# Spreading two small operands over the heads by one set of wide products instead of two sets of narrow ones

## The reference, cut to what matters

```
def _L0_xattn_ref(x, context, W_out, b_out, heads):
    q = x.reshape(b, i, heads, d).transpose(0, 2, 1, 3)
    k = context.reshape(b, j, heads, d).transpose(0, 2, 1, 3)
    v = k
    sim = jnp.einsum('bhid,bhjd->bhij', q, k) * scale
    attn = jax.nn.softmax(sim, axis=-1)
    out = jnp.einsum('bhij,bhjd->bhid', attn, v)
    ...
    return out @ W_out.T + b_out
x = x + _L0_xattn_ref(_layernorm(x, axis=-1), ctx_1024, ...)
x = x + _L0_attn_ref(_layernorm(x, axis=-1), ...)
x = x + _L0_ffn_ref(_layernorm(x, axis=-1), ...)
```

## Time and profile before

| | |
|---|---|
| median of 3 runs | 860.65 us (860.27 to 861.3) |
| the profiled execution | 856.09 us |
| its span, first to last instruction | 854.2 us |
| granted TensorE clock, mean | 0.985 |
| TensorE busy | 764.7 us (90%) |
| VectorE busy | 607.9 us (71%) |
| ScalarE busy | 422.8 us (49%) |
| GpSimd busy | 313.4 us (37%) |

### The profile page before, as it was taken

One profiled execution on the slowest core, in us unless ns is written; L12 is line 12 of the kernel. 1 busy time (PEld: TensorE's weight loads), 2 busy tenths in 40 slices (PEclk: granted clock), 3 DMA queues, 4 the chain that ended last, 5 costly groups with the idle time before them and its releaser, 6 DMA issues.

```text
span 854.2 us, 26663 instructions
## 1 busy us (share of the span) xinstructions
PE 764.7 (90%) x10666; PEld 573.3 (67%) x10666; DVE 607.9 (71%) x1211; ACT 422.8 (49%) x1062; POOL 313.4 (37%) x638
## 2 busy tenths in 40 slices
PE   4798879989898898989989898898988889999998
PEld 2445767768686776867768686786876655666664
DVE  3378687777878778787777877778645566878883
ACT  2344455564646555464564645555332255555552
POOL 2012523324233333333324233333320434786642
PEclk9899999999999999999999999999999899999999
DMA  9945665656547555474555537454061399454430
GB/s 283 316 109 119 140 145 116 141 133 152 137 107 180 125 153 139 109 176 117 137 140 143 140 110 175 125 156 107 3 222 45 129 377 394 159 186 140 143 115 4
DMA packets 113850, 129.17 MB, mean 151 GB/s; under 512 B 13950, under 2 KB 80766, under 8 KB 113728
## 3 DMA queue, kind: packets, MB, share of 16 engines
q1 hardware_dynamic: 105984, 109.35, 48.2%
q0 software_dynamic: 5520, 16.26, 5.6%
q10 hardware_dynamic: 2224, 1.86, 0.8%
HBM read 114.85 MB, written 14.42 MB: 151 GB/s over the span
## 4 chain that ended last, share of the span: by engine, by line
PE 59%; DVE 16%; POOL 7%; issue 7%; ACT 4%; DMA 4%; SPq 3%; DVEq 0%; POOLq 0%
PE bank L499 10%; PE bank L501 8%; PE bank L500 8%; PE bank L1559 8%; PE bank L493 4%; PE scores L550 3%; PE scores L540 3%; PE bank L564 2%; DVE negmax L1030 2%; PE scores L1537 2%; PE scores L1539 2%; PE scores L1538 2%; DMA keys<-in_ctx 2%; POOL soft L1314 2%; PE bank L604 2%
## 5 line engine op out<-in xcount | busy, mean ns | idle before, releaser
L825 ACT ACTIVATE prob<-scores,negmax 128x257 f32<-128x257 f32 x256 | 118.0, 476 | 41.5 <-DVE negmax L1030 40.8
L499 PE MATMUL bank<-qkv_hi,operand_hi 128*128 128x396 f32 x256 | 99.2, 387 | 4.3 <-DVE operand_lo L1034 4.2
L1030 DVE TENSOR_REDUCE negmax<-scores 128x2 f32<-128x514 f32 x128 | 82.1, 683 | 21.8 <-PE scores L540 21.8
L1020 DVE STREAM_TRANSPOSE k_t<-keys 128x512 f32<-128x512 f32 x128 | 88.2, 690 | 12.6 <-DMA keys<-in_ctx 12.5
L500 PE MATMUL bank<-qkv_lo,operand_hi 128*128 128x396 f32 x256 | 88.0, 344 | 0.0
L501 PE MATMUL bank<-qkv_hi,operand_lo 128*128 128x396 f32 x256 | 87.6, 342 | 0.0
L1559 PE MATMUL bank<-w_all,hidden 128*128 x184 | 82.8, 592 | 0.6 <-ACT hidden L1612 0.6
L550 PE MATMUL scores<-consts,prob 128*128 128x128 f32 x512 | 76.7, 273 | 1.6 <-ACT prob L825 1.6
L564 PEld LDWEIGHTS bank<-prob_t,context 128*32 128x32 f32 x4096 | 46.5, 112 | 42.5 <-issue 34.6
L1655 DVE TENSOR_TENSOR w_lo<-w_all,w_hi 128x512 fp32r<-128x512 f32 x89 | 69.2, 836 | 0.2
L550 PEld LDWEIGHTS scores<-consts,prob 128*128 128x128 f32 x512 | 62.5, 143 | 9.6 <-ACT prob L825 2.5
(11 more groups left out here) (249 smaller groups left out, 1718.5 us busy)
## 6 DMA issues: line engine op xcount, KB each, us to landing
keys<-in_ctx SPq DMA_DIRECT2D x256, 128.0 KB, 4.5
context<-in_ctx SPq DMA_DIRECT2D x64, 512.0 KB, 4.6
w_all<-in_L_ffn_W SPq DMA_DIRECT2D x16, 1024.0 KB, 12.8
b<-in_L_ffn_b SPq DMA_DIRECT2D x23, 256.0 KB, 3.6
norm_scratch<-norm SPq DMA_DIRECT2D x16, 256.0 KB, 2.0
x_tile<-in_x SPq DMA_DIRECT2D x8, 256.0 KB, 5.4
x_pair<-in_x SPq DMA_DIRECT2D x8, 256.0 KB, 4.6
x_scratch<-x_tile SPq DMA_DIRECT2D x8, 256.0 KB, 2.5
```

The lines of the kernel that those rows point to most:

```text
L499: pe.matmul(to, op_hi[op][:, c, :], w_hi[name][:, c, columns], start=(c == 0), stop=False)
L825: act.activation(prob[pair][:, gg, :], scores[:, g, 0:J], ACT.Exp, bias=negmax[b % 2][:, g:g + 1], accum_out=sums[t % 2][:, g, bl:bl + 1]) ...
L1020: dve.transpose(dst, src).then_inc(keys_turned, 1)
L1030: dve.tensor_reduce(negmax[b % 2][:, 2 * pair:2 * pair + 2], scores[:, 2 * pair:2 * pair + 2, 0:J], AX.X, ALU.max, negate=True).then_inc(m ...
```

## The change

The two operands of the spread are placed side by side in one tile, `op_both`, so that for each g the 128 columns of `op_plast` stand directly ahead of the 128 of `op_inv`. TensorE makes four products of 256 columns instead of eight of 128: g = 0 and 1 go into bank 0, g = 2 and 3 into bank 2, which is now the physical neighbour of bank 0, so that VectorE reads each half over both banks with one access pattern. One signal, `spread_done`, stands for both; `inv_spread` is gone, and with it VectorE's wait before L1069. The stage `SPREAD_INV` is gone, and `SPREAD` stands at offset 4 instead of 3. Bank 1 is no longer used by the spread. Bank 0 counts as empty once `att_used` is raised (by L1069) instead of `spread_used` (by L1061). GpSimd's `op_inv` waits once for the first bias unit, whose weights share the tile.

```
-    op_plast = late[:, 5, :].rearrange("p (g b i) -> p g b i", g=G, b=BT)
...
-    op_inv = staged_c[:, 0, :].rearrange("p (g b i) -> p g b i", g=G, b=BT)
+    op_both = staged_c[:, 0:2, :].rearrange("p k (g w b i) -> p (k g) w b i", w=2, b=BT, i=S)
+    op_plast, op_inv = op_both[:, :, 0, :, :], op_both[:, :, 1, :, :]
...
+    banks = [stage_banks[:, i, :] for i in (0, 2, 1)]
+    spread_plast, spread_inv = (stage_banks[:, 0:2, :].rearrange("p k (g w n) -> p (k g) w n", w=2, n=P)[:, :, w, :] for w in range(2))
...
-    bank_of = {"queries": 0, "spread": 0, ..., "inv": 1, ...}
+    bank_of = {"queries": 0, "spread": 0, ..., "inv": 2, ...}
...
-    emptied = {..., "spread": spread_used, "inv": att_used, ...}
+    emptied = {..., "spread": att_used, "inv": att_used, ...}
...
             t = tile_at(step, SPREAD)
             if t >= 0:
-                bank = bank_for("spread", t)
                 until.wait_ge(tables_made, 3)
                 until.wait_ge(plast_placed, t + 1)
-                for g in range(G):
-                    done = pe.matmul(bank[:, g * P:(g + 1) * P], samehead[:, g, :, :]...,
-                                     op_plast[:, g, :, :]..., start=True, stop=True)
-                done.then_inc(spread_done, 1)
-            t = tile_at(step, SPREAD_INV)
-            if t >= 0:
-                bank = bank_for("inv", t)
                 until.wait_ge(inv_placed, t + 1)
                 for g in range(G):
-                    done = pe.matmul(bank[:, g * P:(g + 1) * P], samehead[:, g, :, :]...,
-                                     op_inv[:, g, :, :]..., start=True, stop=True)
-                done.then_inc(inv_spread, 1)
+                    if g % 2 == 0:
+                        bank = bank_for(("spread", "inv")[g // 2], t)
+                    done = pe.matmul(bank[:, (g % 2) * 2 * P:(g % 2 + 1) * 2 * P], samehead[:, g, :, :]...,
+                                     op_both[:, g, :, :, :]..., start=True, stop=True)
+                done.then_inc(spread_done, 1)
...
-                dve.tensor_tensor(grid4(att_w), grid4(banks[bank_of["spread"]]), last, ALU.mult).then_inc(spread_used, 1)
+                dve.tensor_tensor(grid4(att_w), spread_plast.rearrange("p g (b i) -> p g b i", b=BT), last, ALU.mult).then_inc(spread_used, 1)
...
-                until.wait_ge(inv_spread, t + 1)
                 until.wait_ge(att_added, t + 1)
-                dve.tensor_tensor(att_w[:, :], att_w[:, :], banks[bank_of["inv"]][:, :], ALU.mult).then_inc(att_used, 1)
+                dve.tensor_tensor(split3(att_w), split3(att_w), spread_inv, ALU.mult).then_inc(att_used, 1)
...
                 until.wait_ge(inverted, t + 1)
-                until.wait_ge(inv_spread, t)
+                until.wait_ge(spread_done, t)
+                until.wait_ge(unit_done, UNITS.index(("bias", 0)) + 1)
```

More of the change, by code:

```diff
@@ L38 @@
 TILE = BT * STEPS
-(INVERT, PLACE_LAST, PLACE_INV, X_BIAS, SPREAD, SPREAD_INV, ATT, ATT_INV, ATT_HI, ATT_LO, XOUT, X1, SCALE1, TURN1, QKV, OUT_BIAS, TURN_Q, TURN_K,
+(INVERT, PLACE_LAST, PLACE_INV, X_BIAS, SPREAD, ATT, ATT_INV, ATT_HI, ATT_LO, XOUT, X1, SCALE1, TURN1, QKV, OUT_BIAS, TURN_Q, TURN_K,
  SELF, SOFT, SOFT_EXP, SOFT_SUM, SOFT_SCALE, SOFT_TURN, SOFT_PLACE, AV, OUT, X2, SCALE3, TURN3, GATE, CHOOSE, RANK,
  QUERIES) = (
-    -5, 0, -5, -6, 3, 3, 3, 4, 4, 2, 10, 17, 19, 21, 24, 26, 41, 41, 45, 46, 46, 50, 48, 56, 55, 63, 83, 89, 86, 95, 105, 105, 118, -54)
+    -5, 0, -5, -6, 4, 3, 4, 4, 2, 10, 17, 19, 21, 24, 26, 41, 41, 45, 46, 46, 50, 48, 56, 55, 63, 83, 89, 86, 95, 105, 105, 118, -54)
 MEASURE_X, SCALE_X = 2 * STEPS + 4, 2 * STEPS + 5
@@ L279, in program @@
     scores = ctx.enter_context(nc.psum_tensor("scores", [P, G, 512], F32))
-    psum = [ctx.enter_context(nc.psum_tensor(f"bank{i}", [P, 512], F32)) for i in range(4)]
-    att_bank, banks = psum[0], psum[1:4]
+    att_bank = ctx.enter_context(nc.psum_tensor("att_bank", [P, 512], F32))
+    stage_banks = ctx.enter_context(nc.psum_tensor("stage_banks", [P, 3, 512], F32))
+    banks = [stage_banks[:, i, :] for i in (0, 2, 1)]
+    spread_plast, spread_inv = (stage_banks[:, 0:2, :].rearrange("p k (g w n) -> p (k g) w n", w=2, n=P)[:, :, w, :] for w in range(2))
     def by_head(t_):
@@ L330, in program @@
     measured_x, rstd_x, normed_x = signal("measured_x"), signal("rstd_x"), signal("normed_x")
-    inverted, plast_placed, inv_placed, spread_done, inv_spread, spread_used, att_added, att_used = (
-        signal(n) for n in ("inverted", "plast_placed", "inv_placed", "spread_done", "inv_spread", "spread_used", "att_added", "att_used"))
+    inverted, plast_placed, inv_placed, spread_done, spread_used, att_added, att_used = (
+        signal(n) for n in ("inverted", "plast_placed", "inv_placed", "spread_done", "spread_used", "att_added", "att_used"))
     att_hi, att_lo = signal("att_hi"), signal("att_lo")
@@ L366, in emptied_unit @@
         return {"down": down_moved, "k": k_summed, "bias": bias_moved}[kind], c + 1
-    bank_of = {"queries": 0, "spread": 0, "xout": 0, "norm": 1, "qkv0": 1, "qkv2": 1, "out": 2, "inv": 1, "gate": 0, "av": 0, "qkv1": 2, "q": 1, "k": 0, "norm3": 1, "rank": 0, "qkv3": 0, "self": 1}
-    step_of = {"queries": QUERIES, "spread": SPREAD, "inv": SPREAD_INV, "xout": XOUT, "norm": TURN1, "qkv0": QKV, "qkv1": QKV + 4, "qkv2": QKV + 8, "qkv3": QKV + 12,
+    bank_of = {"queries": 0, "spread": 0, "xout": 0, "norm": 1, "qkv0": 1, "qkv2": 1, "out": 2, "inv": 2, "gate": 0, "av": 0, "qkv1": 2, "q": 1, "k": 0, "norm3": 1, "rank": 0, "qkv3": 0, "self": 1}
+    step_of = {"queries": QUERIES, "spread": SPREAD, "inv": SPREAD, "xout": XOUT, "norm": TURN1, "qkv0": QKV, "qkv1": QKV + 4, "qkv2": QKV + 8, "qkv3": QKV + 12,
                "q": TURN_Q, "k": TURN_K, "self": SELF, "av": AV, "out": OUT, "norm3": TURN3, "gate": GATE, "rank": RANK}
@@ L376, in stage_step @@
         return step_of[stage] + TILE * (t + 1) + (later_of.get(stage, (0, 0))[t - T + 2] if t >= T - 2 else 0)
-    emptied = {"queries": queries_placed, "spread": spread_used, "inv": att_used, "xout": x1_made, "norm": norm_lo, "q": q2_moved, "self": soft_shifted, "av": self_lo,
+    emptied = {"queries": queries_placed, "spread": att_used, "inv": att_used, "xout": x1_made, "norm": norm_lo, "q": q2_moved, "self": soft_shifted, "av": self_lo,
                "out": x2_made, "norm3": x3_moved, "gate": gate_used, "rank": rank_used}
@@ L621, in stages @@
             if t >= 0:
-                bank = bank_for("spread", t)
                 until.wait_ge(tables_made, 3)
                 until.wait_ge(plast_placed, t + 1)
-                for g in range(G):
-                    done = pe.matmul(bank[:, g * P:(g + 1) * P], samehead[:, g, :, :].rearrange("p h d -> p (h d)"),
-                                     op_plast[:, g, :, :].rearrange("p b i -> p (b i)"), start=True, stop=True)
-                done.then_inc(spread_done, 1)
-            t = tile_at(step, SPREAD_INV)
-            if t >= 0:
-                bank = bank_for("inv", t)
                 until.wait_ge(inv_placed, t + 1)
                 for g in range(G):
-                    done = pe.matmul(bank[:, g * P:(g + 1) * P], samehead[:, g, :, :].rearrange("p h d -> p (h d)"),
-                                     op_inv[:, g, :, :].rearrange("p b i -> p (b i)"), start=True, stop=True)
-                done.then_inc(inv_spread, 1)
+                    if g % 2 == 0:
+                        bank = bank_for(("spread", "inv")[g // 2], t)
+                    done = pe.matmul(bank[:, (g % 2) * 2 * P:(g % 2 + 1) * 2 * P], samehead[:, g, :, :].rearrange("p h d -> p (h d)"),
+                                     op_both[:, g, :, :, :].rearrange("p w b i -> p (w b i)"), start=True, stop=True)
+                done.then_inc(spread_done, 1)
             t, c = part_at(step, XOUT, G)
```

## The result

The changed kernel takes 879.64 us (median; 875.86 to 880.5), the kernel before, measured beside it, 860.97 us. The ratio is 1.0206 [1.0175, 1.0237]: slower, by about 2%, four times what was forecast and outside the range. The profiled execution of the changed kernel takes 880.5 us, its span 878.7 us.

A forecast was written before the change was run, and what follows sets the result against it. TensorE sets the pace overall, but a 9.7 us relay of VectorE, ScalarE and GpSimd bounds this place. The later signal less the saved wait summed to +4.65 us: median 860.65 becomes 865.3 us, range 859.4 to 867.9.

The forecast's parts named there:

- The products: On TensorE, the spread's eight wide passes take 2.00 us; its own work hardly changes.
- the row of equal width: TensorE's fill product of 256 columns in the profile before, giving 0.216 us per further wide pass.
- rival B: In the spread on TensorE, a wide pass costs little more than a narrow one: 859.5 us, chance 0.06.
- The signal: `spread_done` comes 2.00 us after the start instead of 1.16, delaying VectorE's L1061 by +0.29 us in inner tiles.
- Rival C: A handover behind VectorE's third spread operation (L1069) has slack that absorbs the delay: 860.7 us, chance 0.11.
- The wait that goes: VectorE's L1069 has one wait fewer and starts sooner: -0.07 us per tile, 16 times.
- the start: TensorE's spread products wait for one more semaphore: taken as 0, upper bound 0.05 us per tile.
- the operands: GpSimd's placements end 4.9 us before the products need them; VectorE reads banks in pieces of 128 columns: 0.
- The banks: Second half in bank 2: TensorE's stalls of 0.72 and 0.59 us per tile vanish, booked at 0.
- Rival D: With TensorE's stalls merged into one longer pause, the clock might fall to 1.2 GHz: +32 us, 893 us, chance 0.03.

The follow-up runs named there:

- the bank alone: Kernel before, with narrow products and two signals, only the second set of spread products moved from bank 1 to bank 2; 869.65 us, ratio 1.0097.
- the two fills: Two fill products per tile in TensorE's pause: added to the changed kernel, 865.54 us; added to the kernel before with the second set in bank 2, 860.19 us.
- the kernel with the stall kept: Changed kernel with its second half in bank 1 instead of 2, so TensorE waits again for VectorE's softmax subtraction; no fill; 885.53 us, ratio 1.0263.

## Why the prediction was right in its sum and wrong in its time

*The products: right.* 1.99 us, forecast 2.00; the row of equal width decided it, and rival B is refuted.

*The signal: right.* L1059 starts 2.03 us behind the products (forecast 2.04) in all 16 tiles, and the delay passes on whole: pitch +0.21 us, forecast +0.22. Rival C is refuted. That it is the signal's place and not the width, the run with narrow products and a late signal showed.

*The wait that goes, the start, the operands: right.* L1066 follows 0.07 us sooner; VectorE's operations still take 0.69 to 0.70 us. With the pause filled and the clock kept up, the changed kernel takes 865.54 us, where the sum said 865.3; against the kernel beside it that is +4.3 us, forecast +4.65.

*The banks: wrong.* This is the step that failed. It asked what the two stalls cost and rightly found that they lie beside the relay; the run with the bank alone shows that removing them gives no time. But "I book them at 0" asked only whether TensorE could use the time. It did not ask where TensorE's idle time goes. It doesn't vanish: 0.72 + 0.59 us were two pauses between pieces of work, and after the change they are a pause of 0.62 us and one of 1.26 us; only 0.46 us of work separates the longer one from the 0.51 us that TensorE stood before the projection all along. The stretch of 2 us that holds the 1.26 us has 0.46 us of work, and in some of the tiles the clock falls behind it. Measured: some 14 us by wide products (879.64 - 865.54), 8.4 us by the bank alone (869.65 - 861.26). That these falls hang on the new order of TensorE's work is shown in both directions, by the bank alone and by the two fills; what in this order brings one about is not, as the run with a pause of 1.86 us and a full clock shows.

*Rival D had the mechanism, with the wrong price and a chance of 0.03.* Its price took 2 us in each of 16 tiles, +32 us. In fact nine falls came, of 3.4 or 6.8 us, at some 1.0 and 2.6 us each in an inner tile. The reason for its small chance did not hold: the pause of 0.98 us ahead of the spread in t = 0 is one pause in one tile with other work around it, and the clock that it kept did not carry over to the pauses of the other tiles. The earlier trace rows averaged over 10 us, which hides a stretch of 2 us. With a larger chance for D the range would have had to reach up towards its price and taken this case in.

The Trainium skill, "TensorE: Matmul & The Clock Gate", section "A second HAM failure mode: psum-queue depth-cycling", tells of a kernel that cycles through the accumulator banks, and in which short idle times between groups of products bring the clock down again and again. The traces here agree: one bank digit took the mean clock of the profiled execution from 0.985 to 0.969 (0.976 to 0.988 in the runs of before beside it, 0.965 to 0.976 with the digit). The prediction drew on this page for the price of a pass and not for this.

**What stays open.** All 13 inner tiles of the changed kernel have the pause, and only some have the fall, six in the first trace and nine in the second; which ones, and why the longer pause of the kernel with the stall kept brings so few, is not settled. One tile (spread at 263.02 us) has a pitch of 37.35 us at full clock, 0.6 more than its neighbours, 0.35 us of it one stretch in which the chain shows no cause; the changed kernel with fill has such a tile too (403.26 us, 37.47 us).

## What to carry to other kernels

A stall off the critical path is not always free to remove: taking it away reorders TensorE's work, and that can cost the clock. Before taking one away, draw where the idle time will go, and read TensorE's busy time and the granted clock in stretches as short as the pauses. A grown pause did not always bring a fall here, so measure it; where it does, a few products without use in it can cost nothing and keep the clock (here 14 us for two products per tile). When several products share one signal, the first reader pays for the last product; and of two waits ahead of one instruction, write first the one that comes true last.

## What the runs showed of the hardware that was not expected

- A fall to 1.2 GHz came without a long stop of TensorE. It began within a microsecond of the end of stretches of 4 us with 2.03 us (changed kernel), 2.14 us (bank alone) and 2.23 us (changed kernel again) of work, the longest pause in the first 1.26 us, in the second 1.03 us. With that pause filled, 2.76 us of work in 4, the clock stayed at 1.00. But it also stayed at 1.00 in other tiles with the same pause, and in the kernel with the stall kept behind 1.57 us of work in 4 and a pause of 1.86 us.
- In an inner tile of the changed kernel's first trace a fall of 3.4 us cost 1.0 us and one of 6.8 us 2.6 us; with the bank alone a fall of 3.4 us cost up to 1.4 us (37.90 against 36.50). Each is less than half the fall's length, which it would be if TensorE set the pace all through.
- Of two waits ahead of one instruction, the one that comes true last costs some 0.06 us more when it is written second: swapping two lines in two places gave 0.12 us a tile (36.50 to 36.38 us).
